# Layer norm in a four-kind megakernel: GpSimd adds epsilon and subtracts the mean itself, DVE's two small operations are dropped

## What is computed

```python
def _layernorm(x, axis=-1, eps=1e-05):
    m = jnp.mean(x, axis=axis, keepdims=True)
    v = jnp.var(x, axis=axis, keepdims=True)
    return (x - m) / jnp.sqrt(v + eps)
...
x = x + 0.5 * _L0_ffn_ref(_layernorm(x))    # F: 8 experts, 128 -> 512 -> 128, all weighted
x = x + _L0_attn_ref(_layernorm(x))         # R: chunked linear recurrence with a group norm
x = x + 0.5 * _L0_ffn_ref(_layernorm(x))    # F
x = x + 0.5 * _L1_ffn_ref(_layernorm(x))    # E: top 1 of 8 experts, 128 -> 128
x = x + _L1_attn_ref(_layernorm(x))         # M: causal attention, 16 heads of 8
x = x + 0.5 * _L1_ffn_ref(_layernorm(x))    # E
```

## Time and profile before

| | us |
|---|---|
| three timed runs | 1585.59, 1591.86, 1592.55 (median 1591.86) |
| the profiled execution | 1587.52, its span 1585.8 |
| 0 to 540 (first F): PE busy, DVE busy | 524.82, 409.72 |
| 540 to 700 (R): PE, DVE, POOL busy | 142.94, 132.03, 124.59 |
| 700 to 1186 (second F): PE, DVE busy | 485.04, 362.43 |
| 1186 to 1250 (first E): PE, DVE, POOL busy | 54.63, 57.10, 41.04 |
| 1250 to 1508 (M): PE, DVE, POOL busy | 251.07, 241.70, 103.57 |
| 1508 to 1586 (end of M, second E): PE, DVE, POOL busy | 68.58, 61.22, 38.94 |

### The profile page before, as it was taken

The page is one execution under the profiler, slowest core; times in us unless marked ns, Lnnn a source line. Parts: engine busy times, 40 slices in busy tenths (PEclk is TensorE's granted clock), DMA queues, the critical chain, the costliest instruction groups (busy, mean ns, idle before and its releaser), DMA issues. The chain is left out here.

```text
span 1585.8 us, 43554 instructions
## 1 busy us (share of the span) xinstructions
PE 1527.1 (96%) x15760; PEld 910.0 (57%) x15760; DVE 1264.2 (80%) x2662; ACT 934.4 (59%) x1826; POOL 934.7 (59%) x806
## 2 busy tenths in 40 slices
PE   7999999999999899799999999999998899999998
PEld 4666666666666666566666666666663334444443
DVE  7976777777877788786776777768779889999968
ACT  6755555555655433365555555556553378888843
POOL 2865756657664299875756657657446334444454
PEclk9999999999999999999999999999999899999999
DMA  4300000000001243200000000000001212111112
GB/s 163 104 11 5 7 0 7 7 0 7 5 5 34 46 83 76 42 5 5 8 1 7 7 0 7 3 4 8 2 15 28 47 36 61 36 42 46 26 35 67
DMA packets 74636, 43.40 MB, mean 27 GB/s; under 512 B 54106, under 2 KB 71162, under 8 KB 74372
## 3 DMA queue, kind: packets, MB, share of 16 engines
q1 hardware_dynamic: 74500, 41.60, 10.9%
HBM read 10.47 MB, written 2.10 MB: 8 GB/s over the span
## 5 line engine op out<-in xcount | busy, mean ns | idle before, releaser
L642 POOL TENSOR_TENSOR scratch<-scratch 128x512 f16<-128x512 f32 x379 | 440.9, 1164 | 375.4 <-ACT scratch L850 375.0
L845 ACT ACTIVATE scratch<-psum 128x512 f32<-128x512 f32 x512 | 305.2, 597 | 398.0 <-PE psum L2008 397.1
L1420 DVE SCALAR_TENSOR_TENSOR scratch<-psum,scratch 128x512 f32<-128x512 f32 x512 | 352.4, 689 | 234.8 <-PE psum L2008 212.4
L2050 PE MATMUL psum<-ffn_down_hi,scratch 128*128 128x128 f16 x2048 | 369.3, 219 | 0.3
L2051 PE MATMUL psum<-ffn_down_lo,scratch 128*128 128x128 f16 x2048 | 369.4, 219 | 0.0
L2052 PE MATMUL psum<-ffn_down_hi,scratch 128*128 128x128 f16 x2048 | 369.4, 219 | 0.0
L850 ACT ACTIVATE scratch<-scratch 128x512 f16<-128x512 f32 x512 | 318.6, 622 | 9.0 <-DVE scratch L1420 8.9
L2050 PEld LDWEIGHTS psum<-ffn_down_hi,scratch 128*128 128x128 f16 x2048 | 200.3, 98 | 58.9 <-DVE scratch L1427 0.5
L2051 PEld LDWEIGHTS psum<-ffn_down_lo,scratch 128*128 128x128 f16 x2048 | 200.4, 98 | 58.1
L2052 PEld LDWEIGHTS psum<-ffn_down_hi,scratch 128*128 128x128 f16 x2048 | 200.4, 98 | 0.0
L2006 PE MATMUL psum<-x_hi,ffn_gate_hi 128*128 (+1 forms) x512 | 194.5, 380 | 1.5 <-ACT scratch L845 1.5
(11 more groups left out here) (230 smaller groups left out, 2663.7 us busy)
## 6 DMA issues: line engine op xcount, KB each, us to landing
scratch<-scratch SPq DMA_DIRECT2D x96, 128.0 KB, 2.7
raw<-in_ffn_w_dram SPq DMA_DIRECT2D x8, 768.0 KB, 4.3
ffn_up_hi<-scratch SPq DMA_DIRECT2D x32, 128.0 KB, 2.8
x_tok<-in_x_dram SPq DMA_DIRECT2D x8, 256.0 KB, 6.8
out_dram<-x_tok SPq DMA_DIRECT2D x7, 256.0 KB, 2.3
raw<-in_lin_dram SPq DMA_DIRECT2D x1, 1092.0 KB
x_hi<-scratch SPq DMA_TRANSPOSE x46, 2.3
x_lo<-scratch SPq DMA_TRANSPOSE x46, 2.3
```

What stands on the lines that cost most here:

```text
L642: pool.tensor_tensor(h_lo[r], h32[r], h_hi[r], ALU.subtract).then_inc(s_plo, 1)
L845: act.activation(gate_act[k % 2], bank(k % 2), ACT.Silu, scale=W_DOWN).then_inc(s_s, 1)
L1420: dve.scalar_tensor_tensor(h32[k % HSLOTS], bank(5 + k % 2), W_DOWN, gate_act[k % 2], ALU.mult, ALU.mult).then_inc(s_h, 1)
L2050: pe.matmul(dst, h_hi[r][:, cols], hi, start=k % FC == 0 and n == 0, stop=False, skip_group_check=True)
```

## The change

Three things. GpSimd's normalisation in R, E and M takes the mean from `ln_mv` and subtracts it, so `ln_neg` is not needed. In E and M GpSimd itself adds epsilon to the variance, right before the power, and waits for that result; DVE then goes on after `bn_aggr` with its next work. In R and F DVE keeps `ln_var`. Statistics that do not wait for DVE's own aggregates any more get a wait for them ahead (`after`).

```diff
-            def prep_rstd(n):
+            def prep_rstd(n, var=False):
+                if var:
+                    pool.wait_ge(s_mv, n + SUB)
+                    pool.tensor_scalar(ln_var[:], ln_mv[:, 1:2 * SUB:2], LN_EPS, None, ALU.add).then_inc(s_var, SUB)
                 pool.wait_ge(s_var, n + SUB)
                 pool.tensor_tensor(ln_rstd[:], ln_var[:], neg_half[:, 0:SUB], ALU.pow).then_inc(s_rstd, SUB)
...
-                        ins = pool.tensor_scalar(x_norm[:, q * P:(q + 1) * P], sub(x_tok, SUB * (bx % NB) + q), ln_neg[:, q:q + 1],
-                                                 ln_rstd[:, q:q + 1], ALU.add, ALU.mult)
+                        ins = pool.tensor_scalar(x_norm[:, q * P:(q + 1) * P], sub(x_tok, SUB * (bx % NB) + q), ln_mv[:, 2 * q:2 * q + 1],
+                                                 ln_rstd[:, q:q + 1], ALU.subtract, ALU.mult)
...
-            def prep_bn(n, s):
+            def prep_bn(n, s, after=False):
+                if after:
+                    dve.wait_ge(s_mv, n)
                 for q in range(SUB):
                     ins = dve.bn_stats(ln_stat[:, 6 * q:6 * q + 6], sub(x_tok, s + q))
...
-            def prep_aggr(n, negate=False):
+            def prep_aggr(n, var=True):
                 for q in range(SUB):
                     ins = dve.bn_aggr(ln_mv[:, 2 * q:2 * q + 2], ln_stat[:, 6 * q:6 * q + 6])
                 ins.then_inc(s_mv, SUB)
-                dve.wait_ge(s_mv, n + SUB)
-                if negate:
-                    dve.tensor_scalar(ln_neg[:], ln_mv[:, 0:2 * SUB:2], -1.0, None, ALU.mult)
-                dve.tensor_scalar(ln_var[:], ln_mv[:, 1:2 * SUB:2], LN_EPS, None, ALU.add).then_inc(s_var, SUB)
+                if var:
+                    dve.wait_ge(s_mv, n + SUB)
+                    dve.tensor_scalar(ln_var[:], ln_mv[:, 1:2 * SUB:2], LN_EPS, None, ALU.add).then_inc(s_var, SUB)
...
                 def statistics(bx):
                     dve.wait_ge(s_xn, n0 + SUB * bx)
-                    prep_aggr(n0 + SUB * bx, True)
+                    prep_aggr(n0 + SUB * bx, False)
...
                     if stats:
-                        prep_aggr(n0 + SUB * b + SUB * 3, True)
+                        prep_aggr(n0 + SUB * b + SUB * 3)
...
                 def spread(n):
                     dve.wait_ge(s_xn, n)
-                    prep_aggr(n, True)
+                    prep_aggr(n, False)
```

More of the change, by code:

```diff
@@ L112, in build @@
         ln_rstd = sb("ln_rstd", SUB)
-        ln_neg = sb("ln_neg", SUB)
         minus = sb("minus", P, F16)[:]
@@ L712, in moe @@
                 if use:
-                    prep_rstd(n0 + LEAD)
+                    prep_rstd(n0 + LEAD, True)
                     norm(2)
@@ L721, in moe @@
                     if b + 3 < last:
-                        prep_rstd(n0 + SUB * (b + 3))
+                        prep_rstd(n0 + SUB * (b + 3), True)
                         norm(b + 3)
@@ L796, in attention @@
                     mask(u + 1, 1, 2)
-                    prep_rstd(n0 + SUB * b + LEAD)
+                    prep_rstd(n0 + SUB * b + LEAD, True)
                     mask(u + 1, 1, 3)
@@ L1680, in moe @@
                     if what == "spread":
-                        prep_bn(n0 + SUB * b, SUB * b)
+                        prep_bn(n0 + SUB * b, SUB * b, True)
                     if what == "statistics":
@@ L1703, in moe @@
                                 dve.wait_ge(s_mout, b + 4)
-                            prep_bn(n0 + SUB * (b + 3), SUB * ((b + 3) % NB))
+                            prep_bn(n0 + SUB * (b + 3), SUB * ((b + 3) % NB), True)
                         if k == 0 and more:
```

## The result

The changed kernel takes 1609.16 us (median of six runs, 1606.97 to 1614.54) against 1592.12 us for the kernel before (1585.59 to 1592.55): a ratio of the means of 1.0117, 95% interval 1.0096 to 1.0139. A second set of both gave 1610.92 against 1587.34, 1.0145 (1.0115 to 1.0174). Runs of one kernel lie up to 10 us apart, in step with TensorE's mean granted clock: over all sets the kernel before took 1583.7 to 1587.2 us at 0.994 and 1591.4 to 1593.3 at 0.988. So the places of the loss are read from two profiled executions at nearly the same clock: 1610.05 us with a span of 1608.3 after (0.992), against 1587.52 and 1585.8 before (0.993). That is +22.5 us, where +1.3 was forecast; 1609.16 lies above the upper end of the forecast range, 1597.

The account below looks back on a forecast made before the run. The prediction took a circle through DVE and GpSimd to bound Experts, PE to bound Attention. +1.7 us for ten batches less 0.4 made +1.3: 1587.5 to 1588.8 us profiled; it named 1591 us, range 1583.5 to 1597.

Parts of the forecast that it names:

- The step that failed: GpSimd's normalisation: subtracting the mean read from `ln_mv` has the same shape and number of operands, so it costs 0.
- the prediction's own sum: Ten Experts batches held by GpSimd, each 0.17 us longer, +1.7 us; less 0.4 us in the second Experts: +1.3 us.
- The circle through GpSimd and the held L1633: Steady Experts batch: DVE statistics, GpSimd's four steps and the DVE operation waiting for them set its 7.63 us.
- L1633 still ending with the lower half: Experts, sign in the changed trace: this DVE operation still ends with GpSimd's lower half of x.
- The new operation: GpSimd's sum of variance and epsilon, 128x4, in Experts and Attention: 0.34 us, starting the chain 0.17 us later.
- The odd place: Second Experts: comparison L1640, held 1.07 us by GpSimd's addition, might come first and save up to 0.8 us; counted -0.4.
- Attention at 0: Attention: DVE's 0.27 us less work goes into waiting for PE, and the mask has 1.2 us of room: 0.
- DVE's wait of 0.45 us in Attention: Attention, behind the statistics: DVE's wait for PE grows from 0.18 to 0.45 us as 0.27 us of work goes.
- The recurrence's wait: Recurrence: without `ln_neg`, DVE's 0.82 us wait for PE grows by 0.07 us, so the effect is 0.
- The pause between Experts and Attention: Rival: something the rows do not price, such as PE's clock through a changed pause there; both ways, chance 0.06.
- Rival D's price: Experts: GpSimd's sum costs about as much as the power, 1.01 us; 10 x 0.84 = +8.4 us; chance 0.08.

Follow-up runs that it names:

- operand_only: Kernel before, with GpSimd's normalisation taking the mean from `ln_mv` but still adding it; 1588.23 us, ratio 1.0006.
- after_add: Changed kernel with add in place of subtract in GpSimd's normalisation, all else as changed; 1588.29 us, ratio 1.0005.
- eps_only: Changed kernel with `ln_neg` back on DVE and added by GpSimd as before; the sum of epsilon stays on GpSimd; 1589.09 us, ratio 1.0017.
- delay_only: Kernel before, with one more GpSimd power on 128x6 constants ahead of each of the 28 normalisations; 1598.56 us, ratio 1.0067.
- sub_only: Kernel before, with `ln_neg` holding the mean and GpSimd subtracting it in all three normalisations; 1608.13 us, ratio 1.0119.
- m_norm_late: Changed kernel, with Attention's normalisation of the next batch moved behind the four masks of the third group; 1602.53 us, ratio 1.0107.
- attention_add: Changed kernel with add in place of subtract in Attention's normalisation alone; 1604.43 us, ratio 1.0107.

## Why the prediction was wrong

**The step that failed** is the sentence "The normalisation on GpSimd reads the mean from `ln_mv` and subtracts: the same shape and number of operands, 0." The operand costs nothing (0.45 us with either, operand_only 1.0006). The operation costs 0.35 us a tile, 1.40 us a batch. Of all edits it was the one on the longest of GpSimd's steps, and the only one without bounds; the care went into the small operation. Put into the prediction's own sum, 1.40 us more of shift would have read as 10 x 1.4 = +14 us in Experts. That the runs show 13.2 is luck: ten steady batches grow by 0.95 us each over after_add (8.73 against 7.78), 9.5 us, and the rest lies in other batches of the two phases. In its place the runs showed a chain 1.53 us longer, a second held operation in each of the ten held batches and a held join in Attention, some 20 us in all.

**The circle through GpSimd and the held L1633 were right.** What delays GpSimd delays the batch: +0.13 us of shift gave 7.78 us (eps_only), +1.32 gave 8.47, +1.53 in the changed kernel 8.73. The form was not quite right: one us later is not one us longer. With L1633 alone held, GpSimd's end is followed by L1635 and L1640, 0.46 us; once it comes so late that L1640 is the held one, the pick follows at once. So 1.53 us of delay made 1.10 us of batch. "L1633 still ending with the lower half" was wrong in the changed kernel: L1636 ends with the addition, L1643 with the lower half.

**The new operation** was priced 0.34 us and takes 0.233; the gap between it and the power is 0.15 us, not 0.10. The two errors cancel in part: a shift of 0.13 against 0.17 us. after_add, the change without its subtraction, has batches of 7.78 us against the 7.8 forecast, DVE's idle 0.19 us ahead of the pick of tile 0 against 0.2, and +1.0 us in all against +1.3.

**The odd place** in the second Experts: after_add's L1643 never takes more than 0.293 us where L1640 took 1.066 at most before, so DVE does come first there, as the term hoped, and that batch takes 12.05 us in place of 13.12. But the next takes 8.41 in place of 7.62, its L1636 held for 1.06 us, and the phase is no shorter (62.43 against 62.06 us). In eps_only, where only `ln_var` leaves DVE, it stays at 1.092.

**Attention at 0** was right for the two parts that were weighed (after_add's steady batches take 31.28 us, 31.36 before), and wrong in what was not looked at. The masks have an effect on DVE's join, and a late GpSimd alone does not bring it out: delay_only has that, and its joins take 0.30 us and its batches 31.37; in sub_only they take 0.37 and 31.44. Only the changed kernel's subtraction together with its other parts gives joins of 1.08 us and more, and 4.1 of the 6.7 us of Attention in its five steady batches. Why 1.32 us of power ahead of the normalisation leave the join alone, while 1.40 us inside it with the sum and the dropped operations do not, I read from the rows as a matter of 0.1 us: in sub_only the join starts 0.88 us behind the start of the last three masks and ends with the second of them (0.37 us); in the changed kernel it starts 0.75 us behind it and ends with the third. Timelines of DVE and GpSimd, sub_only:

```profile
1337.82 0.37 DVE L1872 TENSOR_TENSOR scratch<-scratch 128x12 f32<-128x12 f32 x1
...
1336.94 1.81 POOL L776 TENSOR_SCALAR_AFFINE_SELECT scratch<-scratch 128x512 f32<-128x512 f32 x3
```

That reading was not tried by itself; m_norm_late and attention_add show that the masks behind the slow normalisation are the cause, not why the join gets through in one kernel and not in the other.

DVE's wait of 0.45 us in Attention did not come either: it stayed at 0.18 (L1899), and 0.16 us went into a wait for ACT ahead of L1895. The recurrence's wait grew from 0.77 to 0.86 us (mean of four), as forecast.

**The pause between Experts and Attention** (E) was not tried; whatever it did lies within the 2 or 3 us by which that stretch scatters.

**Rival D's price**, +8.4 us from GpSimd being 0.84 us later in ten batches, came nearest to what happened, through another operation. It was far off all the same, and no rival was about the normalisation.

## To carry to other kernels

A changed operation code can change the price, even with the same shape and operands: bound it as an added operation is bounded, first on the longest steps of a chain that sets the period. On DVE and GpSimd, ask of every later end which elementwise operation of the other engine, all in SBUF, it will now meet; reductions and work from PSUM were never held here. A batch is best written as stretches between two engines' meetings, with the held time as a term of its own; that sum gave the batches of five kernels to 0.02 us, with the held times read from the traces, and led to the order that is 0.2% faster than before.

## What the hardware showed that was not expected

- GpSimd's `tensor_scalar` with two operations, one of them subtract, takes 3.3 ns a column against 0.83 with add: 0.47 against 0.37 us at 32 columns, 0.82 against 0.45 at 128, 2.08 against 0.77 at 512. Its `tensor_tensor` takes 0.40 us with either.
- With one operation and a scalar for each partition it takes 0.60 us at 128 columns (add, subtract or mult), more than the 0.45 us of add and mult together.
- A DVE `tensor_scalar` with one SBUF input is held by GpSimd (0.22 to 0.84 us), a reduction or reciprocal by none of its six operations tried.
- A GpSimd subtraction of 1.24 us holds DVE for 0.16 us only, and a power of 1.04 us not at all.
